# Expert rows in four equal batches of 128-row units, and gathers held to one per two units

## What is computed

```python
z = layernorm(x)                                  # 8192 x 128
top2, idx = top_k(z @ gate_w + gate_b, 2)         # of 16 experts
share = softmax(top2)
h = relu(z @ w1[e] + b1[e])                       # 128 -> 256, for the two chosen experts
o = h @ w2[e] + b2[e]                             # 256 -> 128
y = z + share[0] * o[first] + share[1] * o[second]
x = x + layernorm(y) * gamma + beta
```

## Time and profile before

| | |
|---|---|
| median of three runs | 1773.17 us (1771.84 to 1773.78) |
| the profiled execution: time / span | 1770.78 us / 1769.0 us |
| PE, ACT, DVE, POOL busy, whole span | 91%, 88%, 85%, 26% |
| granted TensorE clock, mean | 0.971 |
| first result of a unit (L998) / last | 1435.48 us / 1692.40 us |
| first gather (L503) / last | 1524.34 us / 1734.89 us |

### The profile page before, as it was taken

The page is one execution under the profiler, slowest core; times in us unless marked ns, Lnnn a source line. Parts: engine busy times, 40 slices in busy tenths (PEclk is TensorE's granted clock), DMA queues, the critical chain, the costliest instruction groups (busy, mean ns, idle before and its releaser), DMA issues.

```text
span 1769.0 us, 24195 instructions
## 1 busy us (share of the span) xinstructions
PE 1617.3 (91%) x8178; PEld 1065.4 (60%) x8178; DVE 1499.3 (85%) x2298; ACT 1561.5 (88%) x1502; POOL 468.0 (26%) x342
## 2 busy tenths in 40 slices
PE   4999999999999999999999999999999999877710
PEld 3666666666666666565656666666666689767610
DVE  7999999999998989899999898999999845446654
ACT  5899999999999999999999999999999967446521
POOL 0001131222223131304341313041505021364661
PEclk9999999999999999999999999999999999989965
DMA  9559876767667676776766776678767324545531
GB/s 318 154 159 288 232 213 201 208 203 215 196 203 206 205 212 199 208 222 204 211 203 200 210 207 203 198 223 236 212 197 205 115 79 128 169 144 155 150 109 50
DMA packets 216792, 338.22 MB, mean 191 GB/s; under 512 B 18080, under 2 KB 74144, under 8 KB 216544
## 3 DMA queue, kind: packets, MB, share of 16 engines
q1 hardware_dynamic: 208368, 319.62, 61.6%
q0 software_dynamic: 8304, 17.06, 3.2%
HBM read 303.07 MB, written 33.55 MB: 190 GB/s over the span
## 4 chain that ended last, share of the span: by engine, by line
PE 84%; DVE 8%; another core or an unknown queue 3%; issue 3%; ACT 2%; DMA 1%; DVEq 0%; SPq 0%; ACTq 0%
PE acc L1127 49%; PE tp L1146 24%; PE tp L1173 3%; PE tp L1201 2%; PE acc L1201 2%; DVE chunk L663 1%; DVE chunk L1013 1%; DVE stats L675 1%; DVE chunk L669 1%; PE tp L1162 1%; ACT chunk L622 1%; PE misc L1103 1%; DVE msg L738 1%; DMA xs<-in_x_dram 1%
## 5 line engine op out<-in xcount | busy, mean ns | idle before, releaser
L1127 PE MATMUL acc<-wT,msg 128*128 128x512 f32 x2048 | 975.0, 598 | 0.0
L536 ACT ACTIVATE wT<-tp 128x1024 f32<-128x1024 f32 x512 | 758.6, 1668 | 13.8 <-PE tp L1146 12.2
L530 ACT ACTIVATE chunk<-chunk 128x2048 f32<-128x2048 f32 x256 | 653.8, 2554 | 0.1
L669 DVE SCALAR_TENSOR_TENSOR chunk<-chunk 128x2048 f32<-128x2048 f32 x256 | 584.8, 2284 | 54.4 <-ACT chunk L530 53.9
L1146 PEld LDWEIGHTS tp<-ident,chunk 128*128 128x128 f32 x4096 | 477.8, 141 | 223.2 <-issue 221.5
L663 DVE SCALAR_TENSOR_TENSOR chunk<-chunk 128x2048 f32<-128x2048 f32 x256 | 583.5, 2280 | 2.0 <-DMA chunk<-in_adj_dram 2.0
L1146 PE MATMUL tp<-ident,chunk 128*128 128x128 f32 x4096 | 532.9, 273 | 0.0
L525 ACT ACTIVATE chunk<-chunk 128x4096 f32<-128x4096 f32 x118 | 510.4, 4326 | 0.0
L1127 PEld LDWEIGHTS acc<-wT,msg 128*128 128x128 f32 x2048 | 348.6, 190 | 257.6 <-issue 245.2
L462 POOL TENSOR_TENSOR pool_carrier<-pool_carrier 1x1 f32<-1x1 f32 x32 | 44.4, 1388 | 865.8 <-DVE row_now L854 825.6
L483 POOL DMA_INDIRECT rows_in<-y,row_now x128 | 216.7, 1693 | 44.1 <-issue 39.1
(11 more groups left out here) (121 smaller groups left out, 763.9 us busy)
## 6 DMA issues: line engine op xcount, KB each, us to landing
chunk<-in_adj_dram SPq DMA_DIRECT2D x256, 1024.0 KB, 5.4
chunk<-rows_in SPq DMA_DIRECT2D x118, 64.0 KB
rows_out<-chunk SPq DMA_DIRECT2D x59, 128.0 KB
chunk<-rows_in SPq DMA_DIRECT2D x35, 128.0 KB
rows_out<-chunk SPq DMA_DIRECT2D x17, 256.0 KB
y_kept<-y SPq DMA_DIRECT2D x16, 256.0 KB, 6.1
chunk<-y_kept SPq DMA_DIRECT2D x16, 256.0 KB
out_dram<-chunk SPq DMA_DIRECT2D x16, 256.0 KB
```

The source lines that it names most:

```text
L530: act.activation(slot(c), slot(c), ACT.Exp, scale=-1.0).then_inc(inverted, 1)
L536: act.activation(wT[:, (g * PPG + m) % WSLOTS, :], tp[(g * PPG + m) % TSLOTS][:, :], ACT.Exp, scale=-2.0).then_inc(weighted, 1)
L669: dve.scalar_tensor_tensor(out=slot(c), in0=slot(c), scalar=2.0, in1=slot(c), op0=ALU.subtract, op1=ALU.mult).then_inc(squared, 1)
L1127: ins = pe.matmul(acc[:, :], msg[:, n, :], wT[:, (g * PPG + m) % WSLOTS, k * ROWS:(k + 1) * ROWS], start=(n == 0), stop=(n == 2 * PPG - 1))
```

## The change

Three things are changed. The rows go through the experts in four batches of four groups, all in units of 128 rows: four times 47 units, 188 in all. The gathers of all batches stand on one scale: one for every two tiles that go through (`TILES_EACH`), from unit 60 on, and a batch's first no earlier than two units after the batch. Combining starts five units after the release of a group's last gather, and at least six slots after the group before it.

```diff
-    BATCHES = (7, 5, 4)
-    TILES = (1, 2, 1)
+    BATCHES = (4, 4, 4, 4)
+    TILES = (1, 1, 1, 1)
...
-        SCATTER_AT = 52
-
-        def gather_unit(b, nth):
-
-            return min(UNIT0[b + 1] + 2 + nth // TILES[b + 1], NU)
+        SCATTER_AT, TILES_EACH = 52, 2
+        tiles_before = [0]
+        for u in range(NU):
+            tiles_before.append(tiles_before[-1] + TILES[batch_of(u)])
+
+        gather_unit, free = [], 0
+        for b, n in enumerate(BATCHES):
+            free = max(free, tiles_before[max(SCATTER_AT + KB, min(UNIT0[b + 1] + 2, NU))])
+            for _ in range(n * KB):
+                gather_unit.append(min([u for u in range(NU) if tiles_before[u] >= free] + [NU]))
+                free += TILES_EACH
+
...
-        COMBINE_WAIT, COMBINE_PACE, COMBINE_LONG = 8, 6, 11
+        COMBINE_AFTER, COMBINE_PACE, COMBINE_LONG = 5, 6, 11
         starts = []
-        for b, n in enumerate(BATCHES):
-            for _ in range(n):
-                at = UNIT0[b + 1] + COMBINE_WAIT
-                pace = COMBINE_PACE if starts and UR[batch_of(starts[-1])] > P else COMBINE_LONG
-                starts.append(max(at, starts[-1] + pace) if starts else at)
+        for g in range(GROUPS):
+            at = gather_unit[(g + 1) * KB - 1] + COMBINE_AFTER
+            starts.append(max(at, starts[-1] + COMBINE_PACE) if starts else at)
...
-                            pool.wait_ge(ro_ready, gather_unit(b, (g - FIRST[b]) * KB + kb))
+                            pool.wait_ge(ro_ready, gather_unit[g * KB + kb])
```

## The result

The changed kernel takes 1778.39 us (median of six runs, 1776.86 to 1779.56), the kernel before 1773.2 in the same comparison: ratio 1.0025, with a 95% interval of 1.0015 to 1.0035. It is slower, as forecast, but by 0.25% (4.4 us by the ratio, 5.2 between the medians) where 0.55%, 10 us, were forecast. The profiled execution took 1777.67 us, its span is 1775.9.

The account below looks back on a forecast made before the run. PE bounds the kernel until 1428 us; the last 340 us decide. Last result 1677.6, plus 96.4 behind it and 6 for the crawl, gives span 1780.0, put at 1783 us, 0.55% slower; range 1761 to 1808.

Parts of the forecast that it names:

- The stream and units 0 to 58: From the start to unit 58: extra table and pads cost 0 under PE's full time; one more table-register reading costs 0.7 us.
- Rest of table and pads: Slots 59 to 81: 22 slots with table work or pads cost 5 us above the floor, range 3 to 9.
- Combining in the units: Groups 0 to 6 combined beside the units: seven times 5.9 us, 41.3 in all; price range 3.7 to 8.2.
- First gather, gathers, last store: Behind the last unit: 0.6 us to the first gather, 82.1 for 64 gathers, 2.8 for the last store.
- the forecast's case: Own case, chance 0.50: 1777 to 1800 us; four buffers let POOL run four groups ahead, so `back_free` doesn't stop it.
- One last chain: After the last gather lands: the last group's chain, 8.36 us, plus 1.4 for the previous group's two closing steps, 9.7.
- the crawl: DVE slowed behind the units in half the burst: 29 us lost, slack of 3.7 per group against it; 6 us taken.
- DVE and ACT crawl through the whole burst: Rival behind the units: a group takes 23.10 us while gathers run, tail 125 instead of 102, about 1806; chance 0.12.
- "Remote" waits over 20 us would mean that stalls don't come from bursts: Sign in the units: DVE's L998 "remote" waits over 20 us, or a last result after 1692, would contradict bursts causing stalls.
- a tail over 110 says the crawl has spread: Sign behind the last unit: a tail over 110 us would show that DVE's slowing had spread.
- DVE and POOL exclude each other: Rival behind the units: DVE's combining adds to POOL's gather chain, 45 us more, about 1822; chance 0.03.
- DVE doesn't hold them up: Gathers beside DVE's combining: eight take 10.3 us, as in 9.71 while DVE hardly works, so DVE does not delay them.

Follow-up runs that it names:

- one each: The changed kernel with one gather per tile instead of one per two (TILES_EACH 1): 1773.3 us, ratio 0.9999 to the kernel before.
- old rules: The changed kernel's four batches with the earlier gather rule, one per unit, and groups combined 11 slots apart from slot 75: 1777.04 us, ratio 1.0020.
- old batches: The changed kernel with batches of 7, 5 and 4 groups, the second in 256-row units: 1771.34 us at two tiles per gather, 1760.05 at 1.4.
- the pauses: The changed kernel with POOL waiting before groups 11 and 14 until all earlier groups were read by the combining: 1768.59 us, a single run.
- small last batch: The changed kernel with batches of 5, 5, 4 and 2 groups and a gather every 1.2 tiles: 1750.52 us, ratio 0.9869.
- pace 1.3: The changed kernel with batches of 5, 5, 4 and 2 groups and a gather every 1.3 tiles: 1749.14 us, ratio 0.9885.
- dense, spread: The changed kernel with one gather per tile and groups combining 11 slots apart through the units: 1758.67 us, a single run.
- paired: The changed kernel with a gather every 1.4 tiles and groups combining in pairs, 6 slots apart: 1744.5 us, a single run.

## Why the prediction came out as it did

The sign was right, and so was the sense of the exchange: the units gain, the tail loses more. Two of its sizes were wrong, in opposite directions, and nearly cancel. That the total came within 5 us of the forecast is luck: the last result came 23.2 us earlier than the sum had it, the tail was 19.1 us longer, so the span is 1775.9 instead of 1780.0.

- **The stream and units 0 to 58** ("cost 0", 0.7): first result 1435.56 against 1435.48, unit 58 at 1502.25 against the 1502.3 that the sum gives. Right.
- **Rest of table and pads** (5): unit 78 came at 1524.51, 2.3 above the floor. Less than the lower end given for slots 59 to 81.
- **Combining in the units** (7 x 5.9 = 41.3, range from 3.7): this is the step that failed first. From 1502.25 to 1654.41 are 152.2 us, less 129 and 2.3: 20.9 us, or 3.0 per group, under the range. 5.9 was read from a stretch with 9.0 us of "remote" waits in it and eleven gathers to a group, one per unit. At that density it is right (6.2 in the run with one each, 5.6 with groups eleven slots apart, as in that stretch); it was mis-sized because it was taken over to a pace at which it falls by half. The reason given, that in the fourth stretch gathers were already single, took single for sparse. The last result came at 1654.4 instead of 1677.6.
- **First gather, gathers, last store** (0.6, 82.1, 2.8): the first two are right up to the pause; seven groups of eight begin 10 to 11 us apart. The burst lasted 86.9 us, since POOL waited for `back_free` (3.9), which the forecast's case had excluded. The last gather landed 1.5 us later, not 1.2.
- **One last chain** (9.7) and **the crawl** (6): the second step that failed. Four groups were left when the last gather had landed, 29.8 us from 1743.35 to DVE's last instruction. Burst 4.8 more, landing 0.3, chains 20.1, less the 6 allowed: the tail is 19.1 longer than forecast, 121.5. The forecast had counted the slack of 3.7 us per group as if it could be saved up. It can't: DVE spends it waiting for gathers in the first 30 us, and is not ahead when the crawl comes. That was the mechanism of the rival "DVE and ACT crawl through the whole burst", tail 125; only its start was later than the rival had it. (A slip beside it, without weight: 41 us at 14.7 per 20 are 30 lost, not 29.)
- **"Remote" waits over 20 us would mean that stalls don't come from bursts:** they fell from 46.9 to 2.5. But "bursts" is too narrow: single gathers, one per unit, brought 32.9 in the run with one each. And "a tail over 110 says the crawl has spread": it had.
- **DVE and POOL exclude each other:** not by DVE's whole work. Groups of gathers stay 10.0 to 11.0 us apart (1655.0, 1665.0, 1676.0, 1686.8) while DVE combines. But the forecast's "DVE doesn't hold them up" was misread: it set 10.34 us, from group to group, beside 9.71, which ends with the last gather. A gather takes 0.94 us, and longer if it begins while DVE runs L1037 or L1042, the two steps that take two inputs of 128x512 (POOL's timeline, then DVE's):

```profile
1667.57 0.95 POOL L508 DMA_INDIRECT chunk<-rows_out,row_back  x1 [0.30 <-issue]
1668.82 1.36 POOL L508 DMA_INDIRECT chunk<-rows_out,row_back  x1 [0.30 <-issue]
1670.48 1.43 POOL L508 DMA_INDIRECT chunk<-rows_out,row_back  x1 [0.30 <-issue]
```

```profile
1668.67 0.69 DVE L1037 TENSOR_TENSOR chunk<-chunk,gamma_bc 128x512 f32<-128x512 f32 x1
1670.41 0.69 DVE L1042 TENSOR_TENSOR chunk<-chunk,xs 128x512 f32<-128x512 f32 x1
```

Both end 0.8 us behind DVE's instruction, and so does the one at 1726.05 (1.46). Beside L1018 and L680 (1657.65 to 1660.98) gathers keep their 0.94. So the rival is there in small: 2.5 us over the 64 gathers, and not the 45 that it was given.

The sum with the measured terms: 1502.25 + 129 + 2.3 + 20.9 = 1654.4, and 0.57 + 86.86 + 1.51 + 29.79 + 2.76 = 121.5.

Of the change's two parts, four batches alone give 1777.0 (ratio 1.0020), the new rules alone 1771.3 (a single run). The pace of two tiles is the weak number: it leaves 64 gathers for a stretch where nothing covers them. At 1.4 the same kernel takes 1745.8.

## What to carry to other kernels

Work that is spread over a covering stage has a best pace: too dense it stalls the stage, too sparse it is left for the end where nothing hides it; measure the price at two densities before forecasting a third. Slack of an engine that waits for its input can't pay for a slowdown that comes later. Where one engine issues gathers by index for tens of us without a break, look for late instructions on the other engines, and try a pause: here two of 5 us made the tail 10.8 us shorter, in a single run. Set each run against the old kernel timed beside it: on one occasion that kernel itself was 5 us faster.

## What the runs showed of the hardware

- In a long series of gathers by index on POOL, DVE and ACT become late at waits, by 1 to 7 us each. In the changed kernel, DVE's result was there at 1706.3 and ACT's L547, which waits for it, came at 1712.34. The first instruction late by over 1 us had begun to wait 24 us into the burst in the kernel before, 26 to 27 in the changed one, with one each and at the pace of 1.2, 34 at 1.4 and with the old rules, 37 and 38 with the old batches. With the pauses one instruction was late, 27 us into the first of three bursts. In the kernel before and the changed one it lasted until the last gather had landed; with the old batches it ended with a pause of 7.3 us of POOL.
- Bursts of 34 (small last batch), 40 (pace 1.3), 43 (dense, spread) and 50 us (paired) showed nothing, though they are of the same kind. The paired run and the one at 1.4 have the same 37 gathers behind the last result; one crawled. The last three of the four ran on the one occasion on which the kernel before, too, was some 5 us faster. No kernel was traced on both occasions, so it stays open whether the kernel or the occasion decides. The length of a burst matters: the two of 87 and 101 us crawled for more than half of it. What is held up in the chip is open too, and no run tried gathers of fewer rows.
- It is not POOL's being busy (memsets for 50 us: 0.6 us per group), and plain transfers from the same queue did none of it in 35 us.
- A plain transfer takes POOL 0.53 us to issue (4.24 for eight), one by index 1.25 from start to start (0.94 of its own).
- A gather that begins while DVE runs a TENSOR_TENSOR with two 128x512 inputs is held up until 0.8 us after its end: 1.36 and 1.43 us instead of 0.94. SCALAR_TENSOR_TENSOR of 128x128 and the statistics don't do it.
